# Row maxima of four heads at once in four row groups of TensorE, other PSUM rings, masks by matmul, another stage order

## The chip, the cores and the metric

The kernel runs on one core of a Trainium2 chip. The metric is the device time of one execution in microseconds, as the median of several runs. One more execution was recorded by the profiler; its times and rows are used below.

## The reference

Eight images x of 512 tokens by 256 features, each with a context of the same size, go through four decoder-like blocks. All weights and activations are float32. Six attentions stand in the blocks, with 16 heads of 16 features each:

```python
def _mha(qx, kx, ...):                      # attention a = 0..5
    q, k, v = qx @ wq + bq, kx @ wk + bk, kx @ wv + bv      # split into 16 heads of 16
    s = q k^T * scale                       # 512 x 512 scores per head
    # a = 0: s + slope[h] * (j - i), kept where j <= i and i - j < 64      (window)
    # a = 2: kept where j <= i                                            (causal)
    # a = 1, 3, 4, 5: keys from the context, nothing hidden               (full)
    a = softmax(s); return (a @ v) @ wo + bo
```

Around them: x + attention, nine layer norms and three feed-forward networks (256 to 1024 to 256, GELU, GELU, SiLU). The softmax needs each row's largest score ahead of the exponential.

## The kernel before

One program writes all engines' streams from one list of stages, `PLAN`. There are 48 attention loops (8 images by 6 attentions; `LOOPS`, two images in turn). In each loop the kernel does three things side by side:

- Maxima (stage "max", TensorE L670, VectorE L911 or L914). For each head h and each tile i of 128 query rows, TensorE multiplies q with the head's rows kept and all others zeroed (`qm`, made by GpSimd at L1021 for each of 16 heads, in a ring of four) with the 128 rows of `k_high`, in bfloat16, into one PSUM bank of 512 float32. VectorE reduces it to 128 negated row maxima: `tensor_reduce` for a full attention, a custom add-and-reduce with the mask or the bias for the causal and the window one, followed by a read of the accumulator. Of the 64 (head, tile) pairs of a loop each takes one bank of `mx` (three banks, used in turn). Four heads' maxima are turned, written to HBM and read back as a row of `packed["q"]` ("max_rows", "max_back").
- Steps (stages "scores", "values"). A step is a group g of four heads by a tile k of 128 keys, 16 steps in a loop. TensorE makes the transposed scores exactly, from three bfloat16 parts of q and k stacked in 97 rows (106 with the slopes), minus the maximum (L693), into a pair of banks of `st` (two pairs); causal and window steps add a mask by a matmul with the identity for each head (L696, L698). ScalarE takes the exponential of a whole pair, 1024 columns (L829). A step later TensorE multiplies with the values in float32 (L718): 32 columns of the array for each head, four heads side by side, into `pv`.
- The work between: the end of the loop before (output projection, residual, norms, FFN) and the projections of the next. Its float32 matmuls (L645, L654, L731, L742, L768) are recorded as two instructions each. They use the same banks of `st` and `mx`.

A full step of four heads by 128 keys therefore has four score matmuls, the values, and on average four maxima (one query tile of four heads).

Each engine runs its instructions in the order of `PLAN`. A loop has up to four or five streams of stages (steps 0, maxima 1, between 2, context 3, folds 4), and the strings of `MERGE`, one for each kind of loop, say whose stage comes next. `mx_bank` and `st_pair` make TensorE wait until the bank (or pair) that it takes was read by its consumer, which marks `mx_drained` or `st_drained`:

```python
def mx_bank():
    n = jobs["mx"]; jobs["mx"] += 1
    if n >= 3:
        pe.wait_ge(*mx_drained.nth(n - 2))
    return mx[:, n % 3]
```

Of the kernel before, what the change touches and what calls it, by code (L numbers as in the profile page):

```python
# [11 lines left out]
P = 128  # L12
# [11 lines left out]
AHEAD = GRP + 2  # L24
BLK = 32
RING = 4
# [27 lines left out]
def halves(kind, k):  # L54

    q0, q1 = span(kind, k)
    return [range(0, 2), range(2, GRP)] if q1 - q0 > TOK // 2 else [range(GRP)]


def column(kind, k, j):  # L60

    q0, q1 = span(kind, k)
    return j * TOK if len(halves(kind, k)) == 2 else j // 2 * TOK + j % 2 * (q1 - q0)
# [7 lines left out]
def last_half(a, n):  # L71

    return len(halves(ATT_KIND[a], n % TT)) - 1
# [21 lines left out]
TABLES = [("eye", P), ("hide_kq", P), ("hide_qk", TOK), ("whide_kq", WCOL), ("zeros", PAIR), ("wbias_qk", H * WCOL)]  # L95
# [14 lines left out]
LOOPS = [(SLOTS * i + s, a) for i in range(B // SLOTS) for a in range(6) for s in range(SLOTS)]  # L110
LOOP_NO = {ba: j for j, ba in enumerate(LOOPS)}

# [12 lines left out]
def maxima_stages(b, a, heads):  # L125

    for h in heads:
        if h and h + RING - 1 < H:
            yield "mask", b, a, h + RING - 1
        for i in range(TT):  # L130
            yield "max", b, a, h, i
        if h % GRP == GRP - 1:
            yield "max_rows", b, a, h // GRP
        if h % GRP == 0 and h or h == H - 1:
            yield "max_back", b, a, (h - 1) // GRP


def step_stages(b, a):

    yield "load", b, a, 1  # L140
    for n in range(STEPS):
        g, k = divmod(n, TT)
        for e in range(last_half(a, n) + 1):
            yield "scores", b, a, n, e
# [29 lines left out]
def tail_stages(b, a):  # L174

    yield "heads", b, a, NG - 1
    for tag in AFTER[a]:
        if tag[0] == "f":
            f = int(tag[1])
            for c in range(FT // 2):  # L180
                yield "hidden", b, f, c
# [11 lines left out]

def start_stages(b, a):

    yield "project", b, a, "q"
    if own(a):
        yield "project", b, a, "k"
    for h in range(RING):
        yield "mask", b, a, h  # L200
    yield "middle", b, a, "q"
    if own(a):
        yield "middle", b, a, "k"
        yield "project_v", b, a
# [6 lines left out]
def context_stages(b, a):  # L211
# [3 lines left out]
    yield "project", b, a, "k"  # L215
    yield "middle", b, a, "k"
    yield "project_v", b, a
# [19 lines left out]
def streams(j):  # L237

    b, a = LOOPS[j]
    steps, maxima = list(step_stages(b, a)), list(maxima_stages(b, a, range(AHEAD, H)))  # L240
# [11 lines left out]
    "first": "244014414110101114111101101441111011011101141411101100114141011110110114110001410101112122222222"  # L252
           "2220020224424244422424444422040422220040400220024024222042202422004022000",
    "01": "011110111011101112301210111130111011101121122121011212103111011022111011211110011120010222222222"
           "0002222020000222002002202220220200202220002222222",
    "10": "012301230101210122222113112111020101101110112111010111010110010111011010111002100101101011010001"
           "10010012222220222002022202222020200202220200002222200220222200220",
    "11": "011100111101000021100111121012112220202101002211101011210101122220000210112121212221101201101001"
           "0110102011011211000212222220222222020222022022200220220000222002222202222022200",
    "20": "011100211102101111121221222101111200102111102101111211112111121111211101020002222202200102010210"  # L260
           "220110001012122222222222022202220020222000222200202222200220222200022000",
    "21": "023001121011011011011211221222101101120101011100101112301011012111100011121010101100101101011011"
           "312222022222020222020202220020202220220222200220222000222",
# [36 lines left out]
class Signal:  # L300
# [7 lines left out]
    def nth(self, n):  # L308

        return self.sem, n  # L310
# [869 lines left out]
```

## Time and profile before

| what | value |
|---|---|
| median of 3 runs | 3556.03 us (3555.59 to 3560.44) |
| profiled execution, span | 3565.0 us |
| TensorE (PE) busy | 3446.8 us, 97%, 18672 matmul records |
| VectorE (DVE) busy | 2572.8 us, 72% |
| ScalarE (ACT) busy | 1935.0 us, 54% |
| GpSimd (POOL) busy | 1143.4 us, 32% |
| granted TensorE clock, mean | 0.992 of full |

A matmul's busy time includes the way through the array, which the next one overlaps. How much of the engine it takes is told by the distance from one start to the next. PEld is the weight load, which runs beside the matmuls.

### The profile page before, as it was taken

Reading aid. Unit: us, or ns where it says so; the run is one execution under the profiler, and the core shown is the slowest. Engines: PE = TensorE matmul, PEld = TensorE weight load, DVE = VectorE, ACT = ScalarE, POOL = GpSimd, SP = SyncE. Lnnn points to the kernel's source line nnn. Section 1 sums busy time; section 2 is a strip of 40 time slices with the busy share of each in tenths; the row PEclk is TensorE's granted clock in tenths of the full one; section 3 lists DMA queues with packets and bytes.
Section 4 is the critical chain, followed back from the end, with each engine's and each line's share of the span. In section 5 each row is a group of like instructions: output and inputs, shape, how many; then the busy total and the mean of one; then the engine's idle time right before and its main releaser. Section 6 shows DMA issues by size and latency. Waiting matters only on the chain.

```text
span 3565.0 us, 53384 instructions
## 1 busy us (share of the span) xinstructions
PE 3446.8 (97%) x18672; PEld 1657.1 (46%) x18932; DVE 2572.8 (72%) x6523; ACT 1935.0 (54%) x2375; POOL 1143.4 (32%) x1049
## 2 busy tenths in 40 slices
PE   8899999999999999999999999999999999999998
PEld 5545544433454554443354455444335445445333
DVE  5766887756886588766778668777577956976667
ACT  2454565555555456555555545555564654655555
POOL 4322432222532242222253223222235322322222
PEclk9999999999999999999999999999999999999999
DMA  6311321223321231122332122112133312211211
GB/s 213 123 46 55 118 67 54 86 60 93 103 78 43 81 114 46 54 87 60 93 123 74 47 93 82 47 53 87 60 109 110 96 54 81 66 46 63 75 54 55
DMA packets 284317, 280.64 MB, mean 79 GB/s; under 512 B 49858, under 2 KB 275266, under 8 KB 280066
## 3 DMA queue, kind: packets, MB, share of 16 engines
q1 hardware_dynamic: 258324, 274.84, 24.0%
q10 hardware_dynamic: 25728, 2.36, 0.6%
q8 instruction: 154, 2.52, 0.3%
q14 instruction: 111, 0.91, 0.1%
HBM read 195.84 MB, written 81.26 MB: 78 GB/s over the span
## 4 chain that ended last, share of the span: by engine, by line
PE 83%; DVE 11%; issue 2%; ACT 2%; DMA 1%; SPq 1%; POOL 0%; another core or an unknown queue 0%; ACTq 0%; DVEq 0%
PE pv L718 14%; PE st L693 14%; PE mx L670 13%; PE mx L768 10%; PE mx L645 10%; PE st L731 9%; DVE row_max L911 5%; PE mx L742 4%; PE st L654 4%; PE mx L765 2%; PE st L778 2%; DVE mx L914 2%; ACT probs L829 1%; DVE turned L934 1%; DMA rows_of_max_dram<-max_rows 1%
## 5 line engine op out<-in xcount | busy, mean ns | idle before, releaser
L829 ACT ACTIVATE probs<-st 128x1024 f32<-128x1024 f32 (+1 forms) x1344 | 1266.6, 977 | 696.4 <-PE st L693 419.1
L911 DVE TENSOR_REDUCE row_max<-mx 128x1 bf16<-128x512 f32 x2048 | 1283.8, 684 | 216.3 <-PE mx L670 121.0
L1021 POOL TENSOR_TENSOR qm<-q_high,own_rows 128x512 bf16<-128x512 bf16 x768 | 797.3, 1044 | 1583.5 <-PE mx L670 1183.6
L670 PE MATMUL mx<-k_high,qm 128*128 128x512 bf16 (+4 forms) x2812 | 815.2, 342 | 44.7 <-DVE row_max L911 18.2
L693 PE MATMUL st<-q_packed,k_packed 97*128 97x512 bf16 (+2 forms) x3072 | 816.0, 346 | 27.3 <-DMA q_packed<-q_parts_dram 9.9
L718 PE MATMUL pv<-probs,va 128*32 128x512 f32 (+2 forms) x6144 | 701.8, 532 | 12.0 <-ACT probs L829 7.1
L670 PEld LDWEIGHTS mx<-k_high,qm 128*128 128x128 bf16 x3072 | 284.3, 98 | 604.0 <-DVE row_max L911 211.1
L914 DVE CUSTOM_DVE_ANT_0 mx<-mx,tab 128x192 f32<-128x192 f32 (+4 forms) x1024 | 400.9, 444 | 132.4 <-PE mx L670 118.7
L693 PEld LDWEIGHTS st<-q_packed,k_packed 97*128 97x128 bf16 (+1 forms) x3072 | 279.6, 98 | 435.0 <-ACT probs L829 149.8
L731 PE MATMUL st<-xT,w1s 128*128 128x512 f32 x768 | 342.9, 592 | 0.0
L957 DVE TENSOR_TENSOR y<-mx,row 128x256 f32<-128x256 f32 x224 | 94.8, 423 | 299.9 <-PE mx L768 297.2
L1033 POOL TENSOR_TENSOR rstd<-spread_of,m_half 128x2 f32<-128x2 f32 x144 | 100.5, 698 | 586.3 <-DVE spread_of L976 586.3
L718 PEld LDWEIGHTS pv<-probs,va 128*32 128x32 f32 x6144 | 126.1, 108 | 257.9 <-issue 201.8
L844 ACT ACTIVATE hid<-st,col 128x512 f32<-128x512 f32 x192 | 121.6, 685 | 224.3 <-PE st L731 224.3
L768 PE MATMUL mx<-w2s,hid 128*128 128x256 f32 x1024 | 231.6, 379 | 0.0
L731 PEld LDWEIGHTS st<-xT,w1s 128*128 128x128 f32 x768 | 144.7, 190 | 154.3 <-issue 145.4
L768 PEld LDWEIGHTS mx<-w2s,hid 128*128 128x128 f32 x1024 | 189.5, 190 | 23.1
L853 ACT ACTIVATE xT<-st,col 128x256 f32<-128x256 f32 x192 | 97.4, 562 | 174.2 <-PE st L778 123.6
L645 PE MATMUL mx<-xT,sq 128*128 128x512 f32 x352 | 163.9, 611 | 10.2 <-DMA sq<-squares_dram 8.0
L768 PE MATMUL mx<-sq,oT 128*128 128x256 f32 x640 | 166.9, 384 | 0.0
L838 ACT ACTIVATE sums<-pv 128x512 f32<-128x512 f32 x192 | 114.8, 598 | 86.2 <-PE pv L718 58.7
L914 DVE DVE_READ_ACCUMULATOR2_ANT row_max<- 128x1 bf16 x1024 | 147.9, 144 | 0.0
(88 smaller groups left out, 3141.5 us busy)
## 6 DMA issues: line engine op xcount, KB each, us to landing
k_packed<-k_parts_dram SPq DMA_DIRECT2D x576, 128.0 KB, 2.7
q_packed<-q_parts_dram SPq DMA_DIRECT2D x576, 128.0 KB, 2.7
q_parts_dram<-q_low SPq DMA_DIRECT2D x96, 256.0 KB, 2.2
k_parts_dram<-k_low SPq DMA_DIRECT2D x96, 256.0 KB, 2.5
q_parts_dram<-q_high SPq DMA_DIRECT2D x48, 256.0 KB, 2.1
k_parts_dram<-k_high SPq DMA_DIRECT2D x48, 256.0 KB, 2.3
w1s<-w_dram SPq DMA_DIRECT2D x12, 1024.0 KB, 5.1
w2s<-w_dram SPq DMA_DIRECT2D x12, 1024.0 KB, 7.6
```

The lines of the kernel that those rows point to most:

```text
L645: mm = pe.matmul(bank, sqw(f"{m}{a}")[:, j, t * P:(t + 1) * P], src[:, j, :], start=(j == 0), stop=(j == KT - 1))
L654: mm = pe.matmul(pair[:, i // 2, i % 2 * D:(i % 2 + 1) * D], source(b, a)[:, j, i * P:(i + 1) * P], sqw(f"v{a}")[:, j, :], start=(j == 0), ...
L670: mm = pe.matmul(bank[:, 0:k1 - k0], qm[:, h % RING, i * P:(i + 1) * P], high["k"][s][:, t, k0:k1], start=True, stop=True)
L693: mm = pe.matmul(flat[:, c:c + w], kk[:, k * P:(k + 1) * P], qq[:, q0:q1], start=True, stop=(k_kind == FULL))
L718: mm = pe.matmul(pv[j * PAIR:(j + 1) * PAIR, q0:q1], va[s][:, k, at:at + PAIR], probs[:, step % 2, c:c + q1 - q0], start=(k == 0 and k_kin ...
L731: mm = pe.matmul(pair[:, e], w1s[:, j, at:at + P], xT[s][:, j, :], start=(j == 0), stop=(j == KT - 1))
L742: mm = pe.matmul(bank, weight[:, j, t * P:(t + 1) * P], src[:, j, :], start=(j == 0), stop=(j == count - 1))
L768: mm = pe.matmul(bank[:, 0:D], src[:, j, i * P:(i + 1) * P], weight[:, j, :], start=False, stop=(j == count - 1))
L829: act.activation(dst[:, :, 0:w], held["scores", b, a, n, e][:, :, 0:w], ACT.Exp, scale=ATT_SCALE[a]) \
L911: ins = dve.tensor_reduce(top, scores, AX_X, ALU.max, negate=True)
L914: ins = dve.tensor_tensor_reduce(scores, scores, hide[:, hide.shape[1] - (k1 - k0):hide.shape[1]], -1.0, 1e30, ALU.add, ALU.min, top)
L1021: pool.tensor_tensor(qm[:, h % RING], high["q"][s][:, h // HT], own_rows[:, h % HT:h % HT + 1].to_broadcast([P, TOK]), ALU.mult) \
```

## The change

- Maxima: one stage is a query tile of a group of four heads. Four matmuls of 32 rows each, head j in rows 32j to 32j+31 of the array, write into four banks. So q needs masking only as even or odd head in each 32 rows: 4 masked copies for a loop instead of 16 (`slot` says which head that is).
- The causal mask and the window bias of the maxima are added by TensorE (identity times table, four matmuls of 128 rows after the four of 32), and VectorE's custom instruction and accumulator read go. VectorE now reduces two heads in one `tensor_reduce` of 128x2xW, two for a stage.
- PSUM: `st` is three single banks, `mx` two pairs, `pv` one bank. Scores, values projection, FFN and turns take single banks (an exponential reads up to 512 columns). Maxima, projections, rows and adds take pairs; a maxima stage takes both.
- The mask of a causal or window step is one matmul for all heads in a bank.
- "rows": VectorE reads two row tiles in one instruction. Two waits on earlier DMAs come ahead of "middle".
- All `MERGE` strings are new. Maxima run two groups ahead (six heads before).

```diff
-AHEAD = GRP + 2
+AHEAD = 2
-RING = 4
+ONES = 3
+PAIRS = 2
...
+def banks(kind, k):
+    n = per_bank(kind, k)              # TOK // width of the query span
+    return [range(j, min(GRP, j + n)) for j in range(0, GRP, n)]
+def slot(h):
+    return h // HT * HT + h % GRP * 2 + h // GRP % 2
...
-        st = stack.enter_context(nc.psum_tensor("st", [P, 2, 2, TOK], F32))
+        st = stack.enter_context(nc.psum_tensor("st", [P, ONES, TOK], F32))
+        mx = stack.enter_context(nc.psum_tensor("mx", [P, PAIRS, 2, TOK], F32))
         pv = stack.enter_context(nc.psum_tensor("pv", [P, TOK], F32))
-        mx = stack.enter_context(nc.psum_tensor("mx", [P, 3, TOK], F32))
...
+            def ring_pair(signal, name):
+                n = len(pairs_drained)
+                pairs_drained.append(signal.past(name))
+                if n >= PAIRS:
+                    pe.wait_ge(*pairs_drained[n - PAIRS])
+                return mx[:, n % PAIRS]
...
+                    pairs = held["max", b, a, g, i] = [ring_pair(mx_drained, ("max", b, a, g, i, half)) for half in range(2)]
+                    for j in range(GRP):
+                        rows_of = slice(j * PAIR, (j + 1) * PAIR)
+                        mm = pe.matmul(pairs[j // 2][:, j % 2, 0:k1 - k0], qm[rows_of, g, i * P:(i + 1) * P],
+                                       high["k"][s][rows_of, t, k0:k1], start=True, stop=(k_kind == FULL))
+                    if k_kind == CAUSAL:
+                        for j in range(GRP):
+                            mm = pe.matmul(pairs[j // 2][:, j % 2, i * P:(i + 1) * P], tb("eye"), tb("hide_qk"), start=False, stop=True)
+                    if k_kind == WINDOW:
+                        for j in range(GRP):
+                            ...
+                            mm = pe.matmul(pairs[j // 2][:, j % 2, 0:k1 - k0], tb("eye"), ..., start=False, stop=True)
+                    mm.then_inc(*max_filled.mark(("max", b, a, g, i)))
...
+                    for m, j in enumerate(heads):
+                        h = slot(g * GRP + j)
+                        mm = pe.matmul(bank[:, m * w:(m + 1) * w], packed["k"][contracted, h, k * P:(k + 1) * P],
+                                       packed["q"][contracted, h, q0:q1], start=(m == 0), stop=(k_kind == FULL))
+                    if k_kind != FULL:
+                        mm = pe.matmul(to, tb("eye"), hide.unsqueeze(1).to_broadcast([P, len(heads), hide.shape[1]]), ...)
...
+                    dve.wait_ge(*max_filled.past(("max", b, a, g, i)))
+                    for half in range(2):
+                        c = max_column(g * GRP + 2 * half, i)
+                        dve.tensor_reduce(row_max[s][:, c:c + TT + 1:TT], held["max", b, a, g, i][half][:, :, 0:k1 - k0], AX_X, ALU.max,
+                                          negate=True).then_inc(*mx_drained.mark(("max", b, a, g, i, half)))
...
-                    w = (q1 - q0) * len(heads) // 2
+                    w = (q1 - q0) * len(heads)
...
-    "10": "012301230101210122222113112111020101101110112111010111010110010111011010111002100101101011010001"
-           "10010012222220222002022202222020200202220200002222200220222200220",
+    "10": "201000332201000022223010010220010002000100000010100000120010222002102000010000010202000020300200"
+           "1302000000222000000220000020000000200002",
```

## Rows read from the trace of the kernel before

**Rows 1.** The page: busy time of each engine, its share and instructions.

```profile
PE 3446.8 (97%) x18672; PEld 1657.1 (46%) x18932; DVE 2572.8 (72%) x6523; ACT 1935.0 (54%) x2375; POOL 1143.4 (32%) x1049
```

**Rows 2.** Timeline, full loop: start us, us, engine, line, operation, shapes, count.

```profile
181.17 0.38 PE L670 MATMUL mx<-k_high,qm 128*128 128x512 bf16 x1
181.39 0.59 PE L693 MATMUL st<-q_packed,k_packed 97*128 97x512 bf16 x2
...
181.82 0.60 PE L670 MATMUL mx<-k_high,qm 128*128 128x512 bf16 x2
181.87 3.25 DVE L911 TENSOR_REDUCE row_max<-mx 128x1 bf16<-128x512 f32 x5
...
182.34 1.07 PE L718 MATMUL pv<-probs,va 128*32 128x512 f32 x8
...
183.34 0.39 PE L670 MATMUL mx<-k_high,qm 128*128 128x512 bf16 x1
```

**Rows 3.** Timeline: a bank handed from VectorE to TensorE and back, two places.

```profile
278.76 1.89 DVE L911 TENSOR_REDUCE row_max<-mx 128x1 bf16<-128x512 f32 x3
...
279.51 0.39 PE L670 MATMUL mx<-k_high,qm 128*128 128x512 bf16 x1
...
481.56 0.39 PE L670 MATMUL mx<-k_high,qm 128*128 128x512 bf16 x1
...
481.98 0.69 DVE L911 TENSOR_REDUCE row_max<-mx 128x1 bf16<-128x512 f32 x1 [0.24 <-PE mx L670]
```

**Rows 4.** Timeline: eight instructions of a float32 projection.

```profile
474.20 3.60 PE L645 MATMUL mx<-xT,sq 128*128 128x512 f32 x8
```

**Rows 5.** Timeline, window loop: score and mask matmuls in turn, with weight loads.

```profile
135.10 0.22 PE L698 MATMUL st<-tab 128*128 128x128 bf16 x1
...
135.16 0.22 PE L693 MATMUL st<-q_packed,k_packed 106*128 106x128 bf16 x1
...
136.24 0.25 PE L693 MATMUL st<-q_packed,k_packed 106*128 106x192 bf16 x1
136.25 0.10 PEld L698 LDWEIGHTS st<-tab 128*128 128x128 bf16 x1
...
136.33 0.25 PE L698 MATMUL st<-tab 128*128 128x192 bf16 x1
```

**Rows 6.** Groups by form: count, busy us, mean ns, idle before.

```profile
L911 DVE TENSOR_REDUCE row_max<-mx 128x1 bf16<-128x512 f32 x2048 | 1283.8, 684 | 216.3 <-PE mx L670 121.0 <-remote 89.3
L829 ACT ACTIVATE probs<-st 128x1024 f32<-128x1024 f32 x1120 | 1100.5, 1022 | 492.8 <-PE st L693 419.1 <-PE st L696 45.8 <-DVE st L971 11.1
L829 ACT ACTIVATE probs<-st 128x512 f32<-128x512 f32 x64 | 38.2, 597 | 61.1 <-DVE st L971 17.5 <-PE st L698 16.2 <-PE st L696 15.7
L1021 POOL TENSOR_TENSOR qm<-q_high,own_rows 128x512 bf16<-128x512 bf16 x768 | 797.3, 1044 | 1583.5 <-PE mx L670 1183.6 <-ACT q_high L793 317.9 <-remote 81.1
```

**Rows 7.** The masked maxima on VectorE: all forms, two widths alone, accumulator reads.

```profile
L914 DVE CUSTOM_DVE_ANT_0 mx<-mx,tab 128x192 f32<-128x192 f32 (+4 forms) x1024 | 400.9, 444 | 132.4 <-PE mx L670 118.7 <-remote 10.6
...
L914 DVE DVE_READ_ACCUMULATOR2_ANT row_max<- 128x1 bf16 x1024 | 147.9, 144 | 0.0
...
L914 DVE CUSTOM_DVE_ANT_0 mx<-mx,tab 128x192 f32<-128x192 f32 x384 | 134.3, 388 | 38.0 <-PE mx L670 37.6
...
L914 DVE CUSTOM_DVE_ANT_0 mx<-mx,tab 128x512 f32<-128x512 f32 x128 | 92.6, 723 | 14.0 <-remote 10.6 <-PE mx L670 2.6
```

**Rows 8.** Busy time in stretches: stretch, length, PE, PEld, DVE, ACT, POOL, clock, DMA share, GB/s.

```profile
0.00:75.00 75.00, 59.47 (x344) 37.71 (x344) 34.28 (x166) 20.45 (x26) 37.84 (x37) 0.89 0.67 209
170.40:220.40 50.00, 49.11 (x269) 15.36 (x265) 45.55 (x81) 36.21 (x43) 17.74 (x17) 1.00 0.24 73
937.80:981.80 44.00, 39.84 (x389) 26.14 (x381) 34.35 (x171) 19.10 (x26) 28.25 (x26) 0.96 0.43 134
```

**Rows 9.** Who waited for whom: us in total, times, longest.

```profile
PEld mx L670 <- DVE row_max L911: 211.1, 384, 0.9
ACT probs L829 <- PE st L693: 419.1, 373, 14.4
```

More of the change, by code:

```diff
@@ L110 @@
 LOOPS = [(SLOTS * i + s, a) for i in range(B // SLOTS) for a in range(6) for s in range(SLOTS)]
+STRANDS = ["steps", "maxima", "between", "context", "folds"]
 LOOP_NO = {ba: j for j, ba in enumerate(LOOPS)}
@@ L122, in max_column, with keys, maxima_stages @@
     return h // GRP * BLK + h % GRP * TT + i
[L125 to L129, printed above, removed]
-        for i in range(TT):
[L131 to L135, printed above, removed]
+def keys(kind, i):
+    return (max(0, i * P - WIN) if kind == WINDOW else 0), TOK if kind == FULL else (i + 1) * P
+def maxima_stages(b, a, groups):
+    for g in groups:
+        if g + 1 < NG:
+            yield "mask", b, a, g + 1
+        for i in range(TT):
+            yield "max", b, a, g, i
+            if i == 1 and g:
+                yield "max_back", b, a, g - 1
+        yield "max_rows", b, a, g
+    if g == NG - 1:
+        yield "max_back", b, a, g
 def step_stages(b, a):
@@ L142, in step_stages @@
         g, k = divmod(n, TT)
[L143 removed]
+        for e in range(last_bank(a, n) + 1):
             yield "scores", b, a, n, e
@@ L179, in tail_stages @@
             f = int(tag[1])
-            for c in range(FT // 2):
+            for c in range(FT):
                 yield "hidden", b, f, c
@@ L191, in prefetched, with project_stages, value_stages @@
     return a == 0 and b >= SLOTS
+def project_stages(b, a, m):
+    for t in range(KT):
+        yield "project", b, a, m, t
+def value_stages(b, a):
+    for half in range(2):
+        yield "project_v", b, a, half
 def start_stages(b, a):
-    yield "project", b, a, "q"
+    yield from project_stages(b, a, "q")
+    yield "mask", b, a, 0
     if own(a):
-        yield "project", b, a, "k"
-    for h in range(RING):
-        yield "mask", b, a, h
+        yield from project_stages(b, a, "k")
     yield "middle", b, a, "q"
@@ L239, in streams @@
     b, a = LOOPS[j]
-    steps, maxima = list(step_stages(b, a)), list(maxima_stages(b, a, range(AHEAD, H)))
+    steps, maxima = list(step_stages(b, a)), list(maxima_stages(b, a, range(AHEAD, NG)))
     between, context = [], []
@@ new lines, in _ @@
+                    for j in range(KT):
+                        mm = pe.matmul(held["proj", b, a, m][:, t], sqw(f"{m}{a}")[:, j, t * P:(t + 1) * P], src[:, j, :],
+                                       start=(j == 0), stop=(j == KT - 1))
+                    mm.then_inc(*mx_filled.mark(("proj", b, a, m, t)))
+                elif kind == "project_v":
+                    a, half = stage[2:]
+                    if half == 0:
+                        pe.wait_ge(*keys_of(b, a))
+                    bank = held["v", b, a, half] = ring_one(st_drained, ("v", b, a, half))
+                    for i in range(2):
+                        at = (2 * half + i) * P
+                        for j in range(KT):
+                            mm = pe.matmul(bank[:, i * D:(i + 1) * D], source(b, a)[:, j, at:at + P],
```

357 lines of the change are left out of this document (161 added, 196 removed).

## Prediction

> **What bounds the kernel now.** I read the page first: TensorE is busy for 97% of the span, VectorE for 72%, ScalarE for 54% [rows 1]. The share alone doesn't say that TensorE is the limit, since a matmul's record includes its way through the array. So I went to the timeline of a full loop and took distances from start to start. A bfloat16 matmul of 512 columns is recorded with 0.38 us, and the next starts 0.22 us later (181.17 to 181.39) [rows 2]. A float32 one is two instructions of 0.43 us: eight start inside 3.60 us [rows 4]. Masked steps go on at 0.085 us for 192 columns and 0.06 us for 128 [rows 5]. All agree with one column per cycle of 2.4 GHz (0.213 us for 512; float32 twice that, for each of its two instructions) and 2 or 3 ns beside.
>
> The third thing to see is the change of the array's shape. The values use 32 columns per head. Before them the two L670 matmuls from 181.82 stream for 0.43, to 182.25, but the values start at 182.34: 0.09 us lost. They stream 2 x 0.43 = 0.86, and the next matmul starts 1.00 after them: 0.14, of which I put 0.09 to the change back and the rest to the four heads' staggered starts [rows 2].
>
> With these prices and the counts of the stage order I get TensorE's stream before, in us: scores and step masks 618, maxima 550, values 554, rows and their output or FFN matmuls 485, projections 330, FFN up 330, values projection 166, adds 137, turns 112, folding at the start 15: 3297. The order changes between 128x128 and 128x32 1462 times, x 0.093 = 136. Together 3433, and 132 of the 3565 span are left for waits: the start (15 us idle in the first 75), the loops of attention 0 (937.8 to 981.8: TensorE's stream is 34 of 44 us there, for VectorE is busy with masked maxima) [rows 8], and small ones elsewhere. So TensorE is the bound nearly everywhere, and VectorE is close behind in full loops: 45.6 of 50.0 us [rows 8]. TensorE's weight loads wait 211 us for VectorE's maxima, 384 times at 0.55, mostly hidden behind the matmul in flight [rows 9].
>
> **Maxima on TensorE.** Full: 2048 matmuls x 0.216 = 442 us. After: 512 stages, in each four matmuls of 32 rows side by side. No row shows row groups. The nearest is the values' four column groups, where four matmuls take the time of one, plus some 0.02 of stagger [rows 2]. So 0.236 a stage: 121 us, a gain of 321. Bounds: 0.216 (no stagger), or 0.86 (no overlap at all, gain 0). The value by the nearest row is taken. Masked ones: 1024 matmuls, 109 us, become 256 stages of four at once (27 and 5 stagger) and 1024 mask matmuls of 128 rows (67): 99, a gain of 10.
> By the Trainium skill (TensorE: Matmul & The Clock Gate, Part 3, Measured speedup vs the span model) four row tiles of 512 columns gained 3.07 times. A stage would then take 0.28 instead of 0.236, and the sum would be 23 us higher. No run here shows it yet.
>
> **Changes of shape.** The order after has the array go to 32 rows for each maxima stage and back, and I count 2683 changes against 1462: 1221 more x 0.093 = +114 us. Whether a change to row groups costs what the one to column groups costs is not shown: between 0 (+0) and twice (+228, the weights of four groups loaded after the change); I take the measured 0.093. The Trainium skill (TensorEngine Tiling (Array Packing), Key Properties) says that a change of tiling mode drains the engine, which speaks against this change. The 0.09 of [rows 2] agrees.
>
> **Step masks in one matmul.** Columns are the same, some 900 matmuls of 2 to 3 ns beside go: nothing (2 us).
> TensorE's sum: 3433 - 321 - 10 + 114 = 3216, that is -217.
>
> **VectorE.** 684 ns for 512 columns, one each 0.63 (five in 3.25) [rows 2, 6]. Custom forms of 192 and 512 columns differ by 335 ns for 320 columns, so 512 columns are 0.53 and 0.10 is fixed [rows 7]. A pair of banks takes 1.16: 1024 x 1.16 = 1188 for 1284. Masked: 401 + 148 [rows 7] become 512 reduces, 256 causal of 640 columns on average (0.77) and 256 window of 352 (0.46): 315. Rows: 144 instructions fewer, 14. VectorE 2573 - 96 - 234 - 14 = 2229 us. GpSimd: 576 masks fewer x 1.04 = -600 [rows 6], it was off the path. ScalarE: a full exponential 1.94 for two = 0.97; the half as wide is 0.60 alone, about 0.56 back to back, so +0.15 a pair x 1120 = 168, and some 25 for masked steps: 2130 [rows 6]. None of the three reaches TensorE's 3216 in sum, so what they cost is decided step by step.
>
> **The new wait.** A maxima stage takes both pairs, and TensorE waits for both before its first of four matmuls. Maxima can no longer be made while VectorE reduces the ones before. The hand-over is on VectorE's path each time: from the end of the reduce (278.76 + 0.68 = 279.44) to the matmul 0.07, from the matmul to the next reduce 0.42 (481.56 to 481.98) [rows 3], 0.02 stagger and 0.05 of the reduce's end, 0.56 together. What else VectorE has (heads, norms) can fill it where the order has it there. A full step, by engine:
> - TensorE: before 4 x 0.216 + 4 x 0.216 + 1.00 = 2.73; after 0.86 + 1.00 + 0.236 + 0.14 (1.5 further changes) = 2.24.
> - VectorE: before 4 x 0.63 = 2.52; after 2 x 1.16 + 0.56 = 2.88.
> - ScalarE: before 1.94, with a share of the sums 2.09; after 4 x 0.56 + 0.15 = 2.39.
> So where full steps follow each other with little float32 work between (eight loops wholly, some others in part, I put it at 200 of 512 full stages), the step goes from 2.73 to 2.88 and gains nothing: 0.64 of lost time against TensorE's 2.24, of which other work of TensorE covers a quarter, so 0.5 x 200 = +100 us. Where projections, FFN or rows stand between, TensorE stays behind in its stream and VectorE has time: gain kept. Queued behind a waiting maxima stage on TensorE are the scores and values, so ScalarE runs dry too. The three single banks of `st` hold 1.7 us of ScalarE's work where two pairs held 1.9: I put nothing on it, at most 50.
>
> **Sum.** 3565 - 217 + 100 = 3448 of span. The median lies 9 under the profiled span, so 3439.
>
> **Rivals.**
> 1. (0.52) The forecast: 3439.
> 2. (0.20) The hand-over is hidden: the maxima are spread so that TensorE always has a backlog, and the 30 us that loops of attention 0 lose to VectorE's masked maxima go too (3 x 10). 3565 - 217 - 30 - 9 = 3309. For it: TensorE's other work is 2500 us over 768 stages, 3.2 each, more than 2.88. Against it: it isn't evenly spread, FFNs stand in a few loops.
> 3. (0.18) Slower: every maxima stage stalls TensorE by the whole difference, in masked loops too. Price 0.64 in 768 places at most = 490 us; it decides from 217/490 = 44% of the stages on. At 60%: 3565 - 217 + 294 - 9 = 3633. For it: full loops had VectorE busy for 45.6 of 50.0 us already. Against: VectorE's sum falls to 2229.
> 4. (0.07) The four weight loads of 128 columns go one after another at 0.058 each [rows 5], and only from the change on: 3 x 0.058 x 768 = +134, a part of it beside waits for VectorE: 3560. For it: the loads of the values' groups have 32 columns only, these have 128.
> 5. (0.03) The row groups don't run side by side: +331 and no gain left: 3565 + 114 + 100 - 9 = 3770.
>
> **Numbers.** Predicted 3439. The range takes in 2 nearly to its end and the lower part of 3, with 4: 3310 to 3590, leaving out the far part of 3 and 5. Under 0.2% nothing can be told from no change. Faster by more (below 3549): 0.52 + 0.20 + half of 4 = 0.76. Within: 0.03. Slower: 0.21.
>
> **What would show it.** Right: four L670-like matmuls of 32 rows start within 0.02 us, the next stage's change costs 0.09; the tensor_reduce of 1024 columns takes 1.2; in loops such as 170.4 to 220.4 VectorE's idle time before the reduces is released by TensorE, some 0.4 to 0.5 a stage, and TensorE waits for VectorE ahead of the maxima; PE's busy share falls below 95%. Wrong: starts of the four 0.06 apart or more (rival 4), 0.22 apart (5), no idle VectorE before the reduces (2). A granted clock clearly under 0.99 would also break the sum, since TensorE's pauses grow; this I leave out.

## The result, and the profile after

The change made the kernel slower: 3680.7 us (median of four runs, 3674.9 to 3684.8) against 3557.5 for the kernel before beside it, a ratio of 1.034 with a 95% interval of 1.033 to 1.035. The forecast was 3439, the range 3310 to 3590. The profiled execution took 3673.1 us; before it was 3565.0. The median lies 8 us above the profiled span here, where the forecast took it 9 below.

The page answers to [rows 1]: busy time of each engine, its share and its instructions, then the shares of the chain that ended last.

```profile
PE 3343.6 (91%) x19508; PEld 1490.8 (41%) x19508; DVE 2429.0 (66%) x3819; ACT 2104.5 (57%) x3751; POOL 542.6 (15%) x473
...
PE 71%; DVE 18%; ACT 5%; issue 5%; ACTq 1%; POOL 0%; DMA 0%; DVEq 0%; SPq 0%; POOLq 0%
```

VectorE, GpSimd and TensorE are busy for less than before, ScalarE for 170 us more, near the forecast (195 more, to 2130). Yet TensorE's share fell from 97% to 91%, and 18% of the chain now runs through VectorE, where it was 11%. Time went not into work but between it. The trace of before lacks 260 of TensorE's matmuls (18672 for 18932 weight loads [rows 1]), all of them maxima of 512 columns; at 0.216 us each its work was some 56 us larger than its row says.

The groups by form answer to [rows 6] and, with the second row of VectorE, to [rows 7]: count, busy us, mean ns, idle time before them and what ended it.

```profile
L951 DVE TENSOR_REDUCE row_max<-mx 128x2 bf16<-128x1024 f32 x1088 | 1280.8, 1220 | 377.5 <-PE mx L711 357.0 <-PE mx L715 19.5
...
L711 PE MATMUL mx<-k_high,qm 32*128 32x512 bf16 x2176 | 219.7, 391 | 124.8 <-DVE row_max L951 106.2 <-DVE y L994 6.5 <-DVE q_rest L943 6.1
...
L951 DVE TENSOR_REDUCE row_max<-mx 128x2 bf16<-128x1024 f32 (+3 forms) x1536 | 1526.7, 1037 | 553.3 <-PE mx L711 357.0 <-PE mx L715 109.9 <-PE mx L719 85.3
```

2176 matmuls of 32 rows, in 544 groups of four, occupy 219.7 us together, 0.40 a group, so four take the time of one: the row groups work. The idle time of VectorE before its full reduces, with TensorE's maxima as releaser, grew from 121.0 to 357.0 us.

A full loop, as the timeline shows it, answers to [rows 2] and [rows 3]: start us, us, engine, line, shapes, count, idle time before.

```profile
1114.29 0.38 PE L739 MATMUL st<-q_packed,k_packed 97*128 97x512 bf16 x1
...
1114.61 0.40 PE L711 MATMUL mx<-k_high,qm 32*128 32x512 bf16 x4
...
1114.93 1.09 PE L739 MATMUL st<-q_packed,k_packed 97*128 97x512 bf16 x3
1114.99 2.06 ACT L875 ACTIVATE probs<-st 128x512 f32<-128x512 f32 x4
...
1116.04 2.32 DVE L951 TENSOR_REDUCE row_max<-mx 128x2 bf16<-128x1024 f32 x2
...
1118.51 0.40 PE L711 MATMUL mx<-k_high,qm 32*128 32x512 bf16 x4 [0.96 <-DVE row_max L951]
...
1118.95 2.36 DVE L951 TENSOR_REDUCE row_max<-mx 128x2 bf16<-128x1024 f32 x2 [0.28 <-PE mx L711]
...
1121.46 0.40 PE L711 MATMUL mx<-k_high,qm 32*128 32x512 bf16 x4 [0.48 <-DVE row_max L951]
...
1121.90 1.23 DVE L951 TENSOR_REDUCE row_max<-mx 128x2 bf16<-128x1024 f32 x1 [0.59 <-PE mx L711]
```

Read it in three steps. First the change of shape: from the scores at 1114.29 to the maxima is 0.32, of which 0.216 is the stream of 512 columns and 0.10 comes on top; from the maxima to the scores at 1114.93 is 0.32 again. Then the reduces: two take 2.36, or 1.18 each. Then the hand-over: the reduces that end at 1121.31 release the maxima at 1121.46, and those release the next reduce at 1121.90, so 0.59 lie between two pairs of reduces (0.56 was the estimate). A stage of VectorE takes 2.95, against 2.52 for the same four heads before. And TensorE, which has little left to do in that time, sits idle for 0.96 and 0.48.

The waits answer to [rows 9]: us in total, times, longest. The last line is of the kernel before.

```profile
ACT probs L875 <- PE st L739: 507.9, 420, 14.0
PEld st L739 <- ACT probs L875: 413.1, 681, 2.3
DVE row_max L951 <- PE mx L711: 357.0, 383, 5.0
...
PEld mx L711 <- DVE row_max L951: 247.9, 277, 2.9
...
PE mx L711 <- DVE row_max L951: 153.7, 177, 2.6
...
PE st L739 <- ACT probs L875: 63.9, 169, 1.8
```

```profile
PE mx L670 <- DVE row_max L911: 18.2, 68, 0.5
```

Before, TensorE's weight loads waited 211 us for VectorE, 0.55 at a time and mostly behind a matmul in flight. After, a wait lasts 0.9 on the mean, up to 2.9, and 153.7 us of waiting are seen on the matmuls themselves, for 18.2 before. The weight loads' 277 waits fall in 768 maxima stages, so most stages find their banks free. The weight loads of scores wait for exponentials too, 681 times, where it was 225 times and 150 us before. With both pairs in use neither engine works for the other.

Stretches answer to [rows 8]: length, busy us of PE, PEld, DVE, ACT and POOL with counts, granted clock, DMA share, GB/s. The first is a full loop early in the kernel; the last two are the same kind of loop for two of the images, with the same 376 matmuls.

```profile
176.00:238.90 62.90, 53.26 (x312) 19.06 (x308) 50.95 (x68) 40.57 (x77) 9.81 (x9) 0.97 0.23 73
...
1021.60:1077.30 55.70, 45.52 (x376) 23.94 (x368) 41.67 (x68) 25.32 (x49) 7.58 (x8) 0.94 0.26 82
1919.80:1978.10 58.30, 48.12 (x376) 24.96 (x368) 41.65 (x68) 25.41 (x49) 7.56 (x8) 0.88 0.25 78
```

No engine is near the length of any of them: VectorE 51 of 63 us, TensorE 53. Before, a full loop had TensorE busy for 49.1 of 50.0.

### The profile page after: what moved, and what is told of

It is laid out like the page before. It is cut to its first block, busy times and chain, and to the rows that moved or that the text cites. A ratio compares the mean times of both kernels' runs of the same rounds, so it can differ in the third digit from the quotient of the medians.

```text
span 3673.1 us, 54452 instructions
## 1 busy us (share of the span) xinstructions
PE 3343.6 (91%) x19508; PEld 1490.8 (41%) x19508; DVE 2429.0 (66%) x3819; ACT 2104.5 (57%) x3751; POOL 542.6 (15%) x473
## 4 chain that ended last, share of the span: by engine, by line
PE 71%; DVE 18%; ACT 5%; issue 5%; ACTq 1%; POOL 0%; DMA 0%; DVEq 0%; SPq 0%; POOLq 0%
DVE row_max L951 12%; PE pv L765 11%; PE st L739 10%; PE mx L814 10%; PE mx L683 10%; PE st L776 9%; PE mx L711 5%; PE st L694 4%; PE mx L786 4%; ACT probs L875 4%; PE mx L811 2%; DVE y L1019 1%; PE mx L719 1%; PE st L824 1%; PE st L744 1%
## 5 line engine op out<-in xcount | busy, mean ns | idle before, releaser
L875 ACT ACTIVATE probs<-st 128x512 f32<-128x512 f32 (+1 forms) x2624 | 1378.0, 589 | 905.5 <-PE st L739 507.9
L951 DVE TENSOR_REDUCE row_max<-mx 128x2 bf16<-128x1024 f32 (+3 forms) x1536 | 1526.7, 1037 | 553.3 <-PE mx L711 357.0
L739 PE MATMUL st<-q_packed,k_packed 97*128 97x512 bf16 (+2 forms) x3072 | 850.7, 351 | 76.8 <-ACT probs L875 63.9
L739 PEld LDWEIGHTS st<-q_packed,k_packed 97*128 97x128 bf16 (+1 forms) x3072 | 252.8, 98 | 708.4 <-ACT probs L875 413.1
L711 PE MATMUL mx<-k_high,qm 32*128 32x512 bf16 (+2 forms) x3072 | 280.9, 353 | 178.4 <-DVE row_max L951 153.7
L711 PEld LDWEIGHTS mx<-k_high,qm 32*128 32x128 bf16 x3072 | 87.6, 91 | 510.5 <-DVE row_max L951 247.9
L1056 POOL TENSOR_TENSOR qm<-q_high,own_rows 128x512 bf16<-128x512 bf16 x192 | 196.3, 1040 | 505.1 <-ACT q_high L838 496.1
L994 DVE TENSOR_TENSOR y<-mx,row 128x512 f32<-128x512 f32 x112 | 77.5, 692 | 289.2 <-PE mx L814 288.5
L1063 POOL TENSOR_TENSOR k_low<-k_rest,k_low 128x1024 bf16<-128x1024 f32 x48 | 102.2, 2129 | 535.6 <-ACT k_low L845 535.6
L744 PE MATMUL st<-tab 128*128 128x128 bf16 (+3 forms) x576 | 161.3, 280 | 0.0
L970 DVE STREAM_TRANSPOSE turned<-sums 128x512 f32<-128x512 f32 x192 | 134.0, 698 | 14.5 <-ACT sums L883 13.8
```

The source lines that it names most:

```text
L711: mm = pe.matmul(pairs[j // 2][:, j % 2, 0:k1 - k0], qm[rows_of, g, i * P:(i + 1) * P], high["k"][s][rows_of, t, k0:k1], start=True, stop= ...
L739: mm = pe.matmul(bank[:, m * w:(m + 1) * w], packed["k"][contracted, h, k * P:(k + 1) * P], packed["q"][contracted, h, q0:q1], start=(m == ...
L744: mm = pe.matmul(to, tb("eye"), hide.unsqueeze(1).to_broadcast([P, len(heads), hide.shape[1]]), start=False, stop=True)
L875: act.activation(probs[:, step % 2, e * TOK:e * TOK + w], held["scores", b, a, n, e][:, 0:w], ACT.Exp, scale=ATT_SCALE[a]) \
L951: dve.tensor_reduce(row_max[s][:, c:c + TT + 1:TT], held["max", b, a, g, i][half][:, :, 0:k1 - k0], AX_X, ALU.max, negate=True).then_inc(* ...
L1056: pool.tensor_tensor(qm[:, g], high["q"][b % SLOTS][:, t], own_rows[:, odd:odd + 1].to_broadcast([P, TOK]), ALU.mult).then_inc(*pool_step. ...
```

## The experiments

Three theories stood against each other at first. Theory A: the hand-over of both pairs at once stalls TensorE and VectorE in turn, in more stages than the forecast's 200. Theory B: the three single banks of `st` and ScalarE's smaller instructions lose the time. Theory C: the changes of shape do. Each ratio is to the kernel before.

**e1_one_pair: a maxima stage takes one pair of banks, so two stages are in flight.** The matmuls of heads 2 and 3, which ran beside the others, go.

```diff
-pairs = [ring_pair(mx_drained, ("max", b, a, g, i, half)) for half in range(2)]
-for j in range(GRP):
+pairs = [ring_pair(mx_drained, ("max", b, a, g, i, 1))] * 2
+for j in range(2):
```

> The changed kernel, but a maxima stage takes one pair of banks instead of both: only heads 0 and 1 of the four are multiplied (two row groups at once, as long as four), and VectorE reduces the same pair twice. The row maxima of heads 2 and 3 are therefore those of heads 0 and 1, and the scale of the scores is a thousandth so that nothing overflows. The counts of VectorE, ScalarE and of TensorE's changes of shape stay. Theory A (both pairs taken by each maxima stage make a hand-over that neither engine can hide): time falls by 100 to 250 us, to about 3430 to 3580, and VectorE's idle time ahead of the reduces (357 us released by the maxima matmuls) falls to under 100. Theory B (the three single banks of the scores and ScalarE's smaller instructions are the new wait): it falls by less than 50 us. Theory C (the changes of shape alone): no change.

Measured: 3514.7 us, ratio 0.988 (0.986 to 0.989). The page, and the three waits that answer to those above:

```profile
PE 3300.6 (94%) x17972; PEld 1465.2 (42%) x17972; DVE 2420.0 (69%) x3819; ACT 2095.2 (60%) x3751; POOL 543.1 (15%) x473
...
PEld st L739 <- ACT probs L875: 481.6, 801, 2.3
...
DVE row_max L951 <- PE mx L711: 275.5, 280, 5.0
...
PEld mx L711 <- DVE row_max L951: 78.1, 153, 0.9
```

VectorE and ScalarE have the same work, and the stage is as long on TensorE, yet 166 us go. TensorE's waits for maxima fall from 247.9 to 78.1 for the weight loads. Double buffering of the maxima is worth 166 us here. A part of it is the clock: the granted clock is 0.991 again. The time is in Theory A's range, but VectorE's idle time is not: it was to fall under 100 and is 275.5. VectorE still waits for maxima; what is gone is TensorE's waiting for VectorE. And the forecast of a hidden hand-over (3309) isn't reached: another 200 us have another cause, and the weight loads of scores wait even longer for the exponentials (481.6) than in the changed kernel (413.1).

**e2_all_rows: four matmuls of 128 rows, one after another.** TensorE gets 0.65 us more for each full stage, less two changes of shape.

```diff
-rows_of = slice(j * PAIR, (j + 1) * PAIR)
+rows_of = slice(0, P)
```

> The changed kernel, but the four maxima matmuls of a stage take all 128 rows, one after another, and no array change of shape to 32 rows (q's masks are all zero, so the maxima are zero, and the scores' scale is a thousandth). TensorE's stream gets 331 us longer and 1221 changes x 0.098 = 120 us shorter. If TensorE's stream sets the time, 3680 + 211 = 3890. Theory A and B (TensorE waits for VectorE and ScalarE, so its stream has slack): 3680 to 3800, less than half of the 211 appears.

Measured: 3927.2 us, 247 above the changed kernel. The page and three waits:

```profile
PE 3604.0 (92%) x19508; PEld 1690.0 (43%) x19508; DVE 2431.2 (62%) x3819; ACT 2117.3 (54%) x3751; POOL 543.8 (14%) x473
...
DVE row_max L951 <- PE mx L711: 586.6, 430, 5.4
...
PEld mx L711 <- DVE row_max L951: 257.5, 261, 3.0
...
PE mx L711 <- DVE row_max L951: 167.0, 216, 2.5
```

My expectation failed: had VectorE been the limit, TensorE's longer maxima should have been half hidden. They show wholly: TensorE's waits for VectorE are as large as they were (257.5 and 247.9), and VectorE's idle time before the full reduces grows from 357.0 to 586.6. That fits a ring of one buffer, where the maxima are made only while VectorE waits for them, so that their length adds to the cycle. In the stages in which TensorE didn't wait, its longer work adds to the time in any case; the run doesn't part the two. It does show that the row groups pay for themselves: without them this kernel is 247 us slower.

**e5_half_waits: the pairs are taken one by one.** TensorE waits for pair 0, makes heads 0 and 1 and signals, then does the same with pair 1. All heads and masks are computed; the order of the stages is the same.

```diff
+pairs = []
 for j in range(GRP):
+    if j % 2 == 0:
+        pairs.append(ring_pair(mx_drained, ("max", b, a, g, i, j // 2)))
     mm = pe.matmul(pairs[j // 2][:, j % 2, 0:k1 - k0], ...)
+    if j % 2 and k_kind == FULL:
+        mm.then_inc(*max_filled.mark(("max", b, a, g, i, j // 2)))
```

> The changed kernel, but a maxima stage waits for its first pair, multiplies two heads, signals VectorE, and only then waits for the second pair and multiplies the other two. Nothing else is changed, no change of shape is added. Theory A (the hand-over of both pairs at once): VectorE finds its first pair filled while it reduces the second, the idle time ahead of the reduces falls by half or more, and the time falls by 80 to 160 us, to 3520 to 3600. Rival (only two buffers help, as in the run with one pair; TensorE blocks in the stage for the second pair and loses as much as VectorE gains): 3650 to 3690.

Measured: 3606.4 us, ratio 1.014 (1.012 to 1.016), 74 less than the changed kernel. The page and three waits:

```profile
PE 3372.2 (94%) x19508; PEld 1497.6 (42%) x19508; DVE 2423.3 (67%) x3819; ACT 2102.2 (58%) x3751; POOL 542.4 (15%) x473
...
DVE row_max L958 <- PE mx L713: 308.7, 308, 5.0
...
PEld mx L713 <- DVE row_max L958: 198.1, 341, 1.7
...
PE mx L713 <- DVE row_max L958: 75.6, 115, 1.4
```

The waits seen on the matmuls are halved (153.7 to 75.6) though the stream grew a little, since four heads no longer always run side by side. A wait for two resources cost 74 us where one would have done for the first half of the work. This run takes away no work, so the effect can't be put to work left out. It is less than I expected: 80 to 160 us, with VectorE's idle time halved; that time fell only from 357.0 to 308.7.

**e4_two_heads: the same, but the second half of a stage comes two TensorE stages later.** It comes sooner where the next maxima stage or the turning of the maxima stands in between. The order carries (stage, half) pairs, with a wait each.

```diff
+        if stage[0] == "max":
+            yield (*stage, 0)
+            owed, since = (*stage, 1), 0
+            continue
...
+PLAN = list(split_maxima(plan()))
```

> The changed kernel, with each maxima stage in two halves of two heads (two row groups, one pair of banks), the second half at least two TensorE stages after the first. Results as in the changed kernel. TensorE's stream grows by 115 us for the second half and up to 768 x 2 x 0.098 = 150 us of changes of shape. Theory A: the pair is double buffered, the hand-over is hidden, 3500 to 3620 in spite of the longer stream. Theory B: 3700 to 3900.

Measured: 3736.3 us, ratio 1.050, 56 above the changed kernel. The page:

```profile
PE 3540.9 (95%) x19508; PEld 1526.1 (41%) x19508; DVE 2445.4 (66%) x3819; ACT 2108.3 (57%) x3751; POOL 542.5 (15%) x473
```

The halves apart mean 3891 changes of shape for 2683 and twice as many maxima streams: TensorE is busy for 197 us more and its share is 95%. Its matmuls wait 62.0 us for VectorE where it was 153.7, so a part of the hand-over is hidden, and more than that is paid for on TensorE; VectorE's idle time before the full reduces even grows, to 406.7. The time lies in Theory B's range (3700 to 3900) and not in A's, but the longer stream is enough to put it there. Of the two ways of splitting, the one that keeps the halves together (e5) gains.

**e3_singles3 and e7_singles4: the kernel before, its order unchanged, with `st` as three or four single banks and one exponential for each bank.** The two differ by one number.

```diff
+ONES = 3        # e3; 4 in e7
-        st = stack.enter_context(nc.psum_tensor("st", [P, 2, 2, TOK], F32))
+        st = stack.enter_context(nc.psum_tensor("st", [P, ONES, TOK], F32))
```

> The kernel before, with one part of the change alone: the scores, the values projection, FFN and turns use three single banks in turn, and ScalarE reads one bank at a time (stage order, maxima and everything else as before). Theory B: this alone costs 60 us or more (over 3615). Theory A: under 40 us, since TensorE's stream bounds that kernel and ScalarE has 45% idle.

> The kernel before with the scores in single banks as in the run before this one (123 us slower with three), but four of them. If the number of banks is what cost: within 30 us of 3557. If ScalarE's instructions of 512 instead of 1024 columns (0.15 us more a pair): 3620 or more.

Measured: 3682.2 us with three (ratio 1.035) and 3555.4 with four (0.999, 0.998 to 1.000). The weight loads' waits for exponentials, and the matmuls', with three; the last line is the first of them with four:

```profile
PEld st L697 <- ACT probs L836: 432.4, 688, 3.6
...
PE st L697 <- ACT probs L836: 70.5, 165, 3.4
```

```profile
PEld st L697 <- ACT probs L836: 154.2, 228, 0.8
```

So exponentials of half the width cost nothing with four banks, and three banks instead of four cost 127 us in the old order, as Theory B had it. The prediction put nothing, at most 50, on it. That both the changed kernel and e3 stand near 3681 is chance: in e3 the maxima are those of before.

**e6_half_exp: exponentials of at most 256 columns in the changed kernel.** It asks whether ScalarE's speed is what TensorE waits for.

```diff
+                    w = min(w, 256)
```

> The changed kernel, with each exponential cut to the first 256 of up to 512 columns (the other half of the probabilities is left at old values), so ScalarE has about 0.21 us less in each of 2304 and 0.11 in each of 320 instructions, some 500 us in all; banks, order and TensorE's work stay. Theory B (ScalarE and its three banks hold the scores back): the time falls by 60 to 150 us. If only the hand-over of the maxima matters: less than 30 us.

Measured: 3662.1 us, 19 less, for 475 us less of ScalarE's work. The page, and ScalarE's wait for scores (507.9 in the changed kernel):

```profile
PE 3339.3 (91%) x19508; PEld 1499.0 (41%) x19508; DVE 2433.8 (66%) x3819; ACT 1629.9 (45%) x3751; POOL 546.1 (15%) x474
...
ACT probs L876 <- PE st L739: 728.1, 567, 14.4
```

ScalarE waits longer instead. The 19 us are what I expected if its speed isn't the limit. It doesn't clear the banks: the weight loads of scores wait 326.3 us for exponentials where it was 413.1, but those of maxima wait 274.7 for VectorE where it was 247.9, and the clock is 0.976 for 0.980. One wait shrinks and the other takes most of its place.

**e10_scores3 and e10_scores4: the changed kernel with maxima in one bank, so that `st` can have three or four.** The maxima make only head 0, and both reduces read that bank twice.

```diff
-PAIRS = 2
+PAIRS = 1
+top = stack.enter_context(nc.psum_tensor("top", [P, TOK], F32))
...
+                    for j in range(1):
+                        mm = pe.matmul(top[:, 0:k1 - k0], ...)
```

> A control for the next run: the changed kernel with another split of the eight banks. A maxima stage takes one bank of its own (one matmul of 32 rows for head 0, as long as four at once; VectorE reads the bank twice in each of its two reduces, so its work stays), rows and projections take one pair, scores three single banks, values one. The scale of the scores is a thousandth. The hand-over of the maxima is as in the changed kernel, since the next stage waits for both reduces. 3640 to 3760: rows and projections have one pair less and no maxima in it.

> The same with four single banks for the scores. If the fourth bank is worth in the changed kernel what it was in the kernel before (127 us between three and four), this is 80 to 140 us faster than the control. If the new order makes three banks enough: within 30 us of it.

Measured: 3773.5 and 3747.4 us. The waits of the weight loads for exponentials with three and with four banks, and the spans with the mean granted clock:

```profile
PEld st L742 <- ACT probs L878: 426.3, 718, 2.3
...
core 0: 3769.1 us, clock 0.974
```

```profile
PEld st L742 <- ACT probs L878: 277.5, 483, 2.1
...
core 0: 3744.9 us, clock 0.964
```

The control came out slower than its range (3640 to 3760). The fourth bank takes 149 us of waiting away and gives 26 back, not 127; by the condition that I had set, the new order makes three banks enough. The waits say otherwise: with four banks the weight loads of maxima wait 277.4 us for VectorE where it was 226.0 with three, and the clock is 0.01 lower, so what the bank gives is taken up elsewhere. The one pair left also holds rows, adds and projections up in both. What a fourth bank would give the changed kernel isn't shown.

**Orders.** Last, how much the order of the stages hides. New `MERGE` strings come from a search with the durations of the profile as prices, for the changed kernel (e9_order) and for e5 (e8_half_waits_order). Nothing but the strings differs from the changed kernel and from e5.

> The kernel with the two half waits in a maxima stage (3606 us), with all the order strings made anew by a search over orders that counts TensorE's stream, 0.098 for a change of shape, the measured durations of VectorE and ScalarE and the waits for banks. If what is left over the kernel before (48 us) is in the order, the time falls by 80 to 140 us, to 3470 to 3530, under the kernel before. If the banks set it whatever the order: 3580 or more.

> The changed kernel (both pairs waited for at once), with its order strings searched anew in the same way. If its loss of 3.4% is the order's fault: 3560 or less. If it is the hand-over of both pairs in each stage, no order hides it: 3590 to 3650.

Measured: 3578.0 for e8, 28 less than e5, and 3722.9 for e9, 42 more than the changed kernel. Both missed their ranges, e9 badly, and e8's timeline shows a price that the search didn't have:

```profile
1681.04 1.28 ACT L894 ACT_TABLE_LOAD   x1
1682.33 0.69 ACT L894 ACTIVATE hid<-st,col 128x512 f32<-128x512 f32 x1
1683.03 1.28 ACT L882 ACT_TABLE_LOAD   x1
...
1684.33 1.57 ACT L882 ACTIVATE probs<-st 128x512 f32<-128x512 f32 x3
...
1684.98 1.98 PE L783 MATMUL st<-xT,w1s 128*128 128x512 f32 x4 [1.52 <-ACT probs L882]
```

Each FFN tile that stands between exponentials has ScalarE load one table and then the other, 2.57 us, and TensorE waits 1.52 for a bank of `st`. Tables for FFN tiles are loaded 104 times in e8 and 96 times in e9, 48 times in the changed kernel and 24 in the one before. So in a third search a load had the price 1.28. From two starts it gave e11_half_waits_order and e11b_half_waits_order (with e5's waits), and for the changed kernel's own waits e12_order. One of the strings, as it was and as it is in e11:

```diff
-    "20": "010020100022220220201001022002102212121221220022222220000001120020010200212222222122222000200000"
-          "020000000200000020022002200020220000020002",
+    "20": "000200000222221220010022010201122222212211000222220202000120021000102020222222221022220001200000"
+          "200100000200000020202000202020000020002",
```

> The half waits again, with an order searched with ScalarE's table loads counted (1.28 us each time that it goes from exponentials to GELU or back; the order before this one had the FFN's tiles strewn between exponentials). 3480 to 3520, some 2% under the kernel before. If the banks set it whatever the order: 3560 or more.

> Another order from the same search for the half waits (another start), to see how much hangs on the single order: within 20 us of the first, 3480 to 3530.

> The changed kernel, both pairs waited for at once, order searched with the table loads counted. If the loss is the order's: 3560 or less. If the hand-over of both pairs can't be hidden by an order: 3590 to 3650, that is 30 to 90 us better than the changed kernel and still slower than before.

Measured: e11 3482.4 us, ratio 0.979 (0.977 to 0.980); e11b 3491.7, ratio 0.982; e12 3665.5, ratio 1.030. Of e11 the page, the waits for the maxima, the table loads for FFN and the clock; then of e12 the same waits and the clock:

```profile
PE 3344.1 (96%) x19508; PEld 1495.4 (43%) x19508; DVE 2423.8 (70%) x3819; ACT 2132.9 (61%) x3775; POOL 544.2 (16%) x473
...
DVE row_max L958 <- PE mx L713: 228.3, 255, 5.0
...
PEld mx L713 <- DVE row_max L958: 167.7, 366, 1.5
...
L894 ACT ACT_TABLE_LOAD x60 | 77.0, 1283 | 1.1
...
core 0: 3480.6 us, clock 0.995
```

```profile
DVE row_max L951 <- PE mx L711: 374.3, 410, 7.7
...
PEld mx L711 <- DVE row_max L951: 232.0, 307, 2.4
...
core 0: 3661.9 us, clock 0.977
```

Here is the clearest result of the study. The same search gives 124 us with the half waits (3606.4 to 3482.4) and 15 without (3680.7 to 3665.5; I had expected 30 to 90, or more). While both pairs are taken at once, no order found gains much: VectorE's idle time before the full reduces is 357.0 us in the changed kernel, 374.3 in e12 and 461.4 in e9. In e11, with the half waits, it is 228.3, TensorE's share rises to 96%, and the kernel beats the one before by 2.1%, with all of the changed kernel's work (PE busy 3344.1 and 3343.6). That e12 found none doesn't prove that there is none.

## Why the prediction was wrong

**What held.** That the row groups run side by side: the four matmuls take 0.22 of TensorE's time, for the 0.236 forecast, and rival 5 is out. The 0.28 a stage that the forecast mentions beside its sum isn't borne out by this trace. That a change of shape to row groups costs what one to column groups does: 0.10 each way in the timeline above (I take 0.103), against the 0.093 taken, so about 126 us for the forecast's 114; rival 4 would have needed starts 0.058 apart, and a group is recorded with 0.40 for one matmul's 0.38. The Trainium skill (TensorEngine Tiling (Array Packing), Key Properties) says that changing the mode drains the engine; the trace agrees, with 0.10 for each change. That a reduce of 1024 columns takes 1.18 to 1.22. That the hand-over is 0.56 a stage (0.59 measured). And ScalarE's 2130 (2104.5). TensorE's sum then is 3433 - 205 = 3228, near the 3216 of the forecast. The saving in work is real.

**The step that failed: "The new wait".** The span of 3673 less 3228 leaves 445 us in which TensorE doesn't stream at full clock, for 132 before. That is 313 more, where the forecast put 100. The paragraph priced one wait, that of the maxima for VectorE, and put the banks of the scores at nothing. What the 313 are can be estimated from the starts of all matmuls in the traces: each takes one cycle per column at the granted clock (two in float32, as the distances in [rows 4] show), 0.098 us goes to each change of shape, and what is then left before a matmul is put down to what released it or its weight load. In us:

| TensorE's time, an estimate | before | changed | e1 | e5 | e11 | e12 |
|---|---|---|---|---|---|---|
| maxima wait for VectorE's reduces | 68 | 177 | 6 | 92 | 37 | 135 |
| scores wait for exponentials | 4 | 117 | 167 | 120 | 82 | 150 |
| other matmuls that wait for another engine or a DMA | 49 | 102 | 86 | 78 | 51 | 79 |
| streaming at 1.2 GHz, cost | 20 | 57 | 27 | 43 | 14 | 68 |

So the 313 are some 109 for the maxima, 113 for the banks of the scores, 53 for other waits (34 of them of other stages that take a pair of `mx` behind a reduce, and of maxima behind VectorE's other work) and 38 for the clock. Each may be off by some ten us. The term that the forecast put at nothing, at most 50, is as large as the one that it priced, and that is the error. The price of the maxima's wait came out near its 100, in part by luck: not 0.5 us in 200 full stages, but on the mean 0.73 in 243 stages of all kinds, of which the kernel before had 68 us already.

Rival 3, to which I gave 0.18, has the sign and nearly the time (3633 forecast, 3681 measured), but not the way there: it needed the wait in 60% of the stages and 294 us, and the trace shows it in 243 of 768, 32%. The waits also don't add up: e1 takes 171 us of the maxima's away and the scores' grow by 50; e12 takes 42 and the scores' grow by 33. No run here takes both away at once, so the division rests on the traces and not on an experiment. The evidence against a slower kernel was VectorE's sum of 2229, which leads to the second step.

**VectorE's sum.** I took 2229 and it was 2429, and yet the reduces cost what I forecast: 1526.7 us in one group by line, where I had 1188 + 315 = 1503. The error is in the subtraction. I took 401 and 148 for the masked maxima out of the page's 2573 [rows 1, 7], but the records of the custom instruction and of the accumulator read overlap each other, by some 180 us in the trace: all groups of VectorE before add up to 2795, 222 above the page, and after to 2480, 51 above. The groups fall by 315; the page by 144. So VectorE was relieved by less than half of what I reckoned (344), and it had less room for a hand-over of 0.59 than rival 2 supposed.

**Banks for scores.** "I put nothing on it, at most 50." In the old order, having three single banks and not four costs 127 (e3 against e7). My reason, that 1.7 us of ScalarE's work are held where 1.9 were, compared contents and not how a ring of three meets an order that was laid out for pairs: TensorE gets its next bank after each exponential but can be at most three ahead, and FFN tiles and turns take their places in the same ring. By the table it is 113 of the 313, and the same working gives 146 us for e3 and none for e7. In e10 the fourth bank takes it from 120 to 19, while the maxima's wait grows from 151 to 196 and the cost of the clock from 83 to 111: 28 less in sum, close to the 26 that were measured. Weight loads for scores wait 413 us in the changed kernel for 150 before, and still 386 in e11, which is faster than both: that figure holds waits behind a matmul in flight too, so by itself it is no loss.

**The clock.** I left it out, and said that a clock clearly under 0.99 would break the sum. It was 0.980: (1 - 0.980) x 3673 x 2 = 147 us at the lower of the two levels, 1.2 GHz, against 57 before (0.992). Of its 26 falls after the first 80 us, 15 come right behind a stretch in which TensorE didn't stream for more than a third of the time, waiting for VectorE more often than not; the others don't. What it costs can be read from the last two stretches above, in which TensorE waits equally long (17 us each by the starts of its matmuls): at 0.88 the time at 1.2 GHz is 58.3 x 0.24 = 14.0 us, at 0.94 it is 55.7 x 0.12 = 6.7, so 7.3 us more, and the loop is 2.6 longer. At 0.36 us for each, 90 us more are some 32 us, an estimate from one pair of loops; the table's, over the whole trace, is 38. In e1 and e11, which took pauses away, the clock was back at 0.991 and 0.995.

**The sum as it came out.** TensorE's work -205, waits +313: +108 of span, as measured (3565.0 to 3673.1). Against the 313, e5 gains 74 by waiting for one pair at a time, e1 166 by having a second buffer (both with their share of the clock), and e11 198 by half waits and a fitting order, so most of it was no price of the row groups themselves. What stays open is how much a fourth bank for the scores would give once the maxima no longer wait.

The Trainium skill (TensorEngine Tiling (Array Packing), Gotcha 1: PSUM Pressure) says that row tiles write to different banks and so need more of them at a time. The trace agrees in kind: four banks at once leave none for the stage that follows, and e1 puts 166 us on that; and they leave three for the scores, which had four.

## What to carry to other kernels

When a change packs work so that one step takes all buffers of a ring, let each part of the step wait for its own buffer alone: here that, with an order made for it, turned 3.4% slower into 2.1% faster. Price every ring that the change makes smaller, not only the one that it is about: the scores' fourth bank was the payment here, and it was put at nothing. And expect a wait that is taken away to come back in part in the next ring. Busy times of groups can overlap, so a saving must be taken from the page's own total or from distances between starts, never as a group's figure out of the page's.

## What the runs showed of the hardware

- Four matmuls of 32 rows and 512 columns in the four row groups take 0.40 us from the first start to the last end, where one takes 0.38. With the change of shape behind them it is 0.32 from their start to the next matmul; the 0.64 that they save shrink to some 0.44 when they stand alone between matmuls of 128 rows, for they pay two changes.
- A change of shape costs about the same from 128x128 to 32 rows (0.10), back (0.10) and to 32 columns (0.09). There were 2683 of them in the changed kernel, roughly 260 us by these prices, and 3891 in e4.
- ScalarE's exponentials of 512 columns, recorded with 602 ns, go on at 0.5 us one after another (four in 2.06): two of them in 1.08 take little more than one of 1024 columns with its 1.02. Halving the width cost the kernel before nothing with four banks (e7).
- A table load of ScalarE takes 1.28 us, and the next activation starts 0.01 later (1682.33 after 1681.04). In e8, 208 of them were 267 us of ScalarE's time.
- The granted clock differs between orders of the same instructions: with the same 19508 matmuls on TensorE it is 0.995 in e11, 0.986 in e5 and 0.977 in e12. It was lowest, 0.964, in e10_scores4. In the traces it is full or half of 2.4 GHz, nothing between. Which pauses bring it down isn't shown.
